# Second attention: the softmax denominators summed on VectorE instead of in a wide product, one step a batch

## The reference, cut to what matters

```python
q = q * scale
sim = jnp.einsum('bhid,bhjd->bhij', q, k)
attn = _softmax(sim)
out = jnp.einsum('bhij,bhjd->bhid', attn, v)
out = jnp.transpose(out, (0, 2, 1, 3)).reshape(b, n, DIM_INNER)
return out @ w_out
```

## Time and profile before

| | us |
|---|---|
| median of 3 runs | 1093.25 (1093.06 to 1094.26) |
| the profiled execution | 1093.4 |
| its span in the trace | 1091.2 |
| PE busy | 1078.2 |
| DVE busy | 797.2 |
| POOL busy | 796.1 |
| ACT busy | 590.6 |
| PE matmuls of the denominators (L1619) | 128 instructions of 592 ns, which overlap in time |
| DVE inversions (L1955) | 119.5, 128 of 934 ns |

### The profile page before, as it was taken

How to read it: one execution, slowest core, us unless ns; L and a number is a source line. 1 busy time by engine, 2 the same in 40 slices (tenths; PEclk the granted TensorE clock), 3 DMA queues, 4 the chain that set the end, 5 groups by cost and what they waited for, 6 DMA issues and landing times.

```text
span 1091.2 us, 22061 instructions
## 1 busy us (share of the span) xinstructions
PE 1078.2 (99%) x8783; PEld 685.0 (63%) x8783; DVE 797.2 (73%) x1247; ACT 590.6 (54%) x939; POOL 796.1 (73%) x524
## 2 busy tenths in 40 slices
PE   9999999999999999999999999999999999999998
PEld 7898998877745455455455455455455545467886
DVE  4658866476675877877877878878878877895553
ACT  4634453576665555555555555655655655654442
POOL 5789998644467899898898899899899898950000
PEclk9999999999999999999999999999999999999999
DMA  7323333200000000200000000000000000000000
GB/s 257 129 79 99 114 103 99 78 1 1 1 1 2 1 1 2 105 4 1 1 1 1 2 1 2 1 1 2 1 1 2 1 2 1 2 0 11 11 1 20
DMA packets 26870, 31.10 MB, mean 28 GB/s; under 512 B 3345, under 2 KB 23185, under 8 KB 25489
## 3 DMA queue, kind: packets, MB, share of 16 engines
q1 hardware_dynamic: 26448, 29.69, 8.1%
q10 hardware_dynamic: 320, 0.01, 0.0%
HBM read 20.12 MB, written 9.44 MB: 27 GB/s over the span
## 4 chain that ended last, share of the span: by engine, by line
PE 90%; DVE 5%; POOL 2%; ACT 2%; issue 1%; SPq 0%; DMA 0%; DVEq 0%; POOLq 0%; ACTq 0%
PE o_ps L1722 21%; PE mx_ps L1675 7%; PE st_ps L1694 5%; PE st_ps L1700 5%; PE st_ps L1697 5%; PE ha_banks L651 4%; PE bank L2127 3%; PE bank L2129 3%; PE bank L2128 3%; PE mx_ps L1613 3%; PE pj_ps L1627 3%; PE pj_ps L1619 2%; PE ha_banks L704 2%; PE ha_banks L715 2%; PE mx_ps L1607 2%
## 5 line engine op out<-in xcount | busy, mean ns | idle before, releaser
L2040 POOL TENSOR_TENSOR acc<-acc,prob 128x1024 f32<-128x1024 f32 x192 | 468.6, 2441 | 49.0 <-ACT prob L1867 38.8
L1867 ACT ACTIVATE prob<-st_ps 128x1024 f32<-128x1024 f32 x256 | 248.6, 1023 | 197.7 <-PE st_ps L1706 104.0
L1722 PE MATMUL o_ps<-prob,v_cur 128*64 128x512 f32 x1024 | 246.4, 602 | 0.0
L1930 DVE TENSOR_REDUCE mx_part<-mx_ps 128x1 f32<-128x512 f32 x258 | 164.8, 666 | 58.0 <-PE mx_ps L1675 58.0
L1933 DVE TENSOR_REDUCE mx_part<-mx_ps 128x2 f32<-128x1024 f32 x78 | 93.6, 1200 | 62.0 <-PE mx_ps L1675 62.0
L1722 PEld LDWEIGHTS o_ps<-prob,v_cur 128*64 128x64 f32 x1024 | 63.8, 136 | 108.9 <-issue 72.8
L1955 DVE RECIPROCAL rden<-rden 128x128 f32<-128x128 f32 x128 | 119.5, 934 | 0.0
L1675 PEld LDWEIGHTS mx_ps<-k_hi,q_hi 64*128 64x128 f32 x414 | 46.5, 183 | 106.7 <-issue 72.6
L1675 PE MATMUL mx_ps<-k_hi,q_hi 64*128 64x512 f32 x414 | 111.9, 457 | 1.2 <-DVE mx_part L1933 0.6
L2040 POOL TENSOR_TENSOR acc<-prob 128x1024 f32<-128x1024 f32 x32 | 76.7, 2397 | 33.9 <-ACT prob L1867 33.3
L1700 PE MATMUL st_ps<-q_hi,d_lo 64*128 64x512 f32 x512 | 100.9, 390 | 0.0
(11 more groups left out here) (414 smaller groups left out, 2266.2 us busy)
## 6 DMA issues: line engine op xcount, KB each, us to landing
v_rows<-ha_v SPq DMA_DIRECT2D x8, 1024.0 KB, 4.1
ha_vt<-v_rows SPq DMA_DIRECT2D x16, 512.0 KB, 4.0
q_max<-mx_turned SPq DMA_DIRECT2D x128, 1.0 KB
h_w<-in_h SPq DMA_DIRECT2D x2, 1024.0 KB, 8.0
w_raw<-in_w SPq DMA_DIRECT2D x8, 192.0 KB, 3.4
head_wkv<-in_wkv SPq DMA_DIRECT2D x2, 512.0 KB, 5.8
m_w<-in_m SPq DMA_DIRECT2D x3, 256.0 KB, 2.9
out<-fin SPq DMA_DIRECT2D x3, 256.0 KB, 2.2
```

The source lines that it names most:

```text
L1722: mm = pe.matmul(o_ps[rows(h), :], v_cur[:, m % 2, j, rows(h)], prob[:, (16 * m + slot) % RING, h, :], start=(j == 0), stop=(j == KT - 1), ...
L1867: act.activation(prob[:, n % RING, :, :], st_ps[:, slot % 2, :, :], ACT.Exp, scale=SCALE).then_inc(s_exp, 1)
L1930: dve.reduce_max(mx_part[:, h, i, keys:keys + 1], maxima_banks(q, n)[h], AX_X).then_inc(s_mxr, 1)
L2040: pool.tensor_tensor(total, old, new, ALU.add).then_inc(s_acc, 1)
```

## The change

The denominator is now made in these pieces, for each half of each step:

1. turn: VectorE transposes `acc` [128 x 1024] in blocks of 32x32 into `turned`;
2. sum: VectorE sums each 32 columns of `turned`, which gives `den_part` [128 x 32];
3. PE multiplies `den_part` (16 columns a head) with `lanes`, a matrix that adds up the four blocks of 32 partitions and repeats the result, 4 records of 16 columns in the place of 4 of 512;
4. ACT copies 128x16 to `den_out` in the place of 128x512;
5. back: VectorE inverts 128x16, and transposes it, repeated 32 times, into `rden` [128 x 512].

The places move. VectorE: turn of half 1 (of the step before) in batch 1, its sum in 2, back in 3; turn of half 0 in batch 4, sum in 5, back in 6; both normalisations now in 6 (half 1 of the step before) and 7 (half 0 of this step). PE: the den of half 1 goes from batch 1 to 2, that of half 0 stays in batch 5. POOL's first add of a half now waits for the turn, not for the product. The order after the last step is another: "out" of half 0 comes where the last den stood, the last den after the first hidden layer, the last "out" after two blocks of the second.

```diff
+    LANES, DEN = 32, CH // 32
+    turned = early.sb("turned", [P, 2 * CH])
...
-    INVERT = {6: (0, 0, 0), 7: (0, 1, 0), 0: (0, 2, -1), 1: (0, 3, -1),
-              2: (1, 0, -1), 3: (1, 1, -1), 4: (1, 2, -1), 5: (1, 3, -1)}
+    DEN_TURN, DEN_SUM, DEN_BACK = {1: (1, -1), 4: (0, 0)}, {2: (1, -1), 5: (0, 0)}, {3: (1, -1), 6: (0, 0)}
+    NORMALIZE = {6: (1, -1), 7: (0, 0)}
...
-    AFTER = {1: ("den", 1), 3: ("out", 0), 5: ("den", 0), 7: ("out", 1)}
+    AFTER = {2: ("den", 1), 3: ("out", 0), 5: ("den", 0), 7: ("out", 1)}
+    AFTER_END = {1: ("out", 0), 2: ("den", 1), 7: ("out", 1)}
...
         elif u[0] == "den":
-            half = u[1]
-            pe.wait_ge(s_acc, ADDS * q + 7 * (half + 1))
+            pe.wait_ge(s_turns, den_done(q, u[1], "summed"))
             for h in range(2):
-                mm = pe.matmul(pj_ps[rows(h), :], c.ones[:, 0:HD], acc[:, half, h, :],
+                mm = pe.matmul(pj_ps[rows(h), 0:DEN], lanes[:, :], den_part[:, h * DEN:h * DEN + DEN],
                                start=True, stop=True, skip_group_check=True)
...
-            act.activation(rden[:, half, :], pj_ps[:, :], ACT.Copy).then_inc(s_den, 1)
+            act.activation(den_out[:, :], pj_ps[:, 0:DEN], ACT.Copy).then_inc(s_den, 1)
...
+    def vector_den_turn(dve, q, half):
...
+        dve.wait_ge(s_acc, ADDS * q + 7 * (half + 1))
+        dve.transpose(turned[:, :], acc[:, half, :, :].rearrange("p h n -> p (h n)")).then_inc(s_turns, 1)
+
+    def vector_den_sum(dve, q, half):
+        dve.wait_ge(s_turns, den_done(q, half, "turned"))
...
+        dve.reduce_sum(den_part[:, :], turned[:, :].rearrange("p (n r) -> p n r", r=LANES), AX_X).then_inc(s_turns, 1)
+
+    def vector_den_back(dve, q, half):
+        dve.wait_ge(s_den, 2 * q + half + 1)
+        if q:
+            dve.wait_ge(s_on, 2 * (q - 1) + half + 1)
+        dve.reciprocal(den_rcp[:, :], den_out[:, :]).then_inc(s_turns, 1)
+        dve.wait_ge(s_turns, den_done(q, half, "inverse"))
+        dve.transpose(rden[:, half, :].rearrange("p (n r) -> p n r", r=LANES),
+                      den_rcp[:, :].unsqueeze(2).to_broadcast([P, DEN, LANES])).then_inc(s_turns, 1)
...
-        vector_invert(dve, m, b)
+        if den_at(DEN_SUM, m, b):
+            vector_den_sum(dve, *den_at(DEN_SUM, m, b))
         at_b = before(m, b)
         if second:
             vector_maxima(dve, *second)
         if at_b and at_b[1][0] == "qk":
             vector_low(dve, *at_b)
-        if b == 1 and m >= 1:
-            vector_normalize(dve, m - 1, 0)
-        if b == 5 and m >= 1:
-            vector_normalize(dve, m - 1, 1)
+        if den_at(DEN_TURN, m, b):
+            vector_den_turn(dve, *den_at(DEN_TURN, m, b))
+        if den_at(DEN_BACK, m, b):
+            vector_den_back(dve, *den_at(DEN_BACK, m, b))
+        if den_at(NORMALIZE, m, b):
+            vector_normalize(dve, *den_at(NORMALIZE, m, b))
...
             if m:
-                pool.wait_ge(s_pj, count_of[m - 1, ("den", half)])
+                pool.wait_ge(s_turns, den_done(m - 1, half, "turned"))
```

More of the change, by code:

```diff
@@ L1422, in second_attention, with den_done @@
     ADDS = 14
-    RCPS = 4
-    INVERT = {6: (0, 0, 0), 7: (0, 1, 0), 0: (0, 2, -1), 1: (0, 3, -1),
-              2: (1, 0, -1), 3: (1, 1, -1), 4: (1, 2, -1), 5: (1, 3, -1)}
+    DEN_STEPS = {name: n + 1 for n, name in enumerate(("turned", "summed", "inverse", "back"))}
+    def den_done(q, half, name):
+        return len(DEN_STEPS) * (2 * q + half) + DEN_STEPS[name]
+    DEN_TURN, DEN_SUM, DEN_BACK = {1: (1, -1), 4: (0, 0)}, {2: (1, -1), 5: (0, 0)}, {3: (1, -1), 6: (0, 0)}
+    NORMALIZE = {6: (1, -1), 7: (0, 0)}
     QK = (("qk", 1, 0), ("qk", 0, 0), ("qk", 0, 1), ("qk", 1, 1))
@@ L1454, in after @@
     def after(m, b):
-        if b not in AFTER:
-            return None
-        q = m + AHEAD[AFTER[b]]
-        return (q, AFTER[b]) if 0 <= q < STEPS else None
+        places = AFTER if m < STEPS else AFTER_END
+        if b not in places:
+            return None
+        q = m + AHEAD[places[b]]
+        return (q, places[b]) if 0 <= q < STEPS else None
     def maximum(m, b, second):
@@ L1825, in scalar_unit @@
             half = u[1]
[L1826 to L1827 removed]
+            if q or half:
+                was = 2 * q + half - 1
+                act.wait_ge(s_turns, den_done(was // 2, was % 2, "inverse"))
             act.wait_ge(s_pj, count_of[q, u])
[L1829 removed]
+            act.activation(den_out[:, :], pj_ps[:, 0:DEN], ACT.Copy).then_inc(s_den, 1)
     def scalar_differences(act, q):
@@ L1891, in vector_start @@
         dve.memset(mx_part[:, :, :, :], 0.0).then_inc(s_rowfill, 1)
+        for h in range(2):
+            dve.reduce_sum(lanes[:, h * LANES:h * LANES + LANES], c.ident[:, :].rearrange("p (n r) -> p r n", r=LANES), AX_X)\
+               .then_inc(s_rowfill, 1)
     def vector_split(dve, p):
@@ L1944, in vector_maxima, with den_at @@
             dve.transpose(mx_turned[:, :], mx_row[:, :].bitcast(F32)).then_inc(s_turned, 1)
[L1946 to L1955, removed]
+    def den_at(places, m, b):
+        if b not in places or m == STEPS:
+            return None
+        half, ahead = places[b]
+        return (m + ahead, half) if 0 <= m + ahead < STEPS else None
+    def vector_den_turn(dve, q, half):
+        if q or half:
+            was = 2 * q + half - 1
+            dve.wait_ge(s_turns, den_done(was // 2, was % 2, "summed"))
+        dve.wait_ge(s_acc, ADDS * q + 7 * (half + 1))
+        dve.transpose(turned[:, :], acc[:, half, :, :].rearrange("p h n -> p (h n)")).then_inc(s_turns, 1)
+    def vector_den_sum(dve, q, half):
+        dve.wait_ge(s_turns, den_done(q, half, "turned"))
+        if q or half:
+            dve.wait_ge(s_pj, count_of[(q, ("den", 0)) if half else (q - 1, ("den", 1))])
+        dve.reduce_sum(den_part[:, :], turned[:, :].rearrange("p (n r) -> p n r", r=LANES), AX_X).then_inc(s_turns, 1)
[7 more added lines that the diff above has]
+                      den_rcp[:, :].unsqueeze(2).to_broadcast([P, DEN, LANES])).then_inc(s_turns, 1)
     def vector_normalize(dve, q, half):
@@ L1960, in vector_normalize @@
         dve.wait_ge(s_osum, 2 * q + half + 1)
-        dve.wait_ge(s_rcp, RCPS * (2 * q + half + 1))
+        dve.wait_ge(s_turns, den_done(q, half, "back"))
         dve.tensor_tensor(o_n[:, half, :], o_sum[:, half, :], rden[:, half, :], ALU.mult).then_inc(s_on, 1)
@@ L1984, in vector @@
         was = (m, b - 1) if b else (m - 1, BATCHES - 1)
-        if after(*was) and AFTER[was[1]][0] == "out":
+        if after(*was) and after(*was)[1][0] == "out":
             vector_add_out(dve, *after(*was))
@@ L2465, in _ @@
                 t2.tensor(pe, STEPS, 1)
[L2466 to L2470, removed]
+                for m in range(HT):
+                    end.tensor_hidden(pe, 0, 1, m)
+                t2.tensor(pe, STEPS, 2)
                 end.tensor_hidden(pe, 0, 2, 0)
+                end.tensor_hidden(pe, 0, 2, 1)
                 t2.tensor(pe, STEPS, 7)
@@ L2479, in _ @@
                         for m in range(HT):
-                            if (k, layer) != (0, 1) and (k, layer, m) != (0, 2, 0):
+                            if (k, layer) != (0, 1) and (k, layer, m) not in ((0, 2, 0), (0, 2, 1)):
                                 end.tensor_hidden(pe, k, layer, m)
```

24 lines of the change are left out of this document (16 added, 8 removed).

## The result

The changed kernel takes 1102.91 us (median of four executions, 1101.22 to 1104.72) against 1093.76 us for the kernel before (1093.06 to 1094.34): ratio 1.0084, 95% interval 1.0065 to 1.0103. It is slower by 9.15 us. The forecast was +23.4. The profiled execution of after is the longest of its four, 1104.72 us, with a span of 1102.5 us.

The account below looks back on a forecast made before the run. PE, busy 99%, was taken to bound the kernel if DVE and POOL deliver; step 0 -0.6, steps 1 to 7 and 14 +9.6, steps 8 to 13 +9.2, last step +5.8, after it -0.6: +23.4 on 1093.4, 1117 us; range 1082 to 1125.

Parts of the forecast that it names:

- The 0.05 us a step for batches 1 and 4: DVE, batches 1 and 4: turns end within 0.2 us of the next first set, costing 0.05 us a step.
- The mechanism: Batch 6: the normalisation misses POOL's add boundary by 0.36 us, waits for that add, and PE waits 2.37 us.
- The wait of the last step: Last step: PE's den waits 5.5 us for DVE's sum, queued behind x_hi, x_lo and h_lo; 1.8 to 6.9 possible.
- +5.2 for the last step and the end: Last step +5.8 from the den's wait, dens and tiles left to split; after it -0.6 for a cheaper last den.
- By the same sum it misses by a hair: Steps 8 to 13, batch 6: normalisation ready 0.03 us after POOL's add begins, so +1.53 a step, +9.2 in all.
- rival (a): Steps 8 to 13: the normalisation gets in ahead of POOL's add, -5.7 there; +8.5 in all, 1102 us; chance 0.20.
- Step 7: Booked with steps 1 to 7 and 14: batch 6's normalisation waits for POOL's add, +1.2 us a step.
- Steps 1 to 6 and 14: Booked with step 7: -1.22 for dens, +0.05 for batches 1 and 4, +2.37 for PE's wait; +1.2 a step.
- rival (e): Last step: PE's clock falls in the long wait, slowing the matmuls behind; +2 to +4 us on any case, no chance given.
- (b): Batch 6, all steps: the normalisation gets in ahead of POOL's add, the way back being shorter; 1085 us; chance 0.18.
- (c): Whole kernel: DVE has room everywhere and PE's saving of 19.5 us is all there is; 1074 us; chance 0.07.
- (d): Batches 1 and 4: turns cost 0.057 us per 32 columns and overrun, +1.35 a step; 1136 us; chance 0.08.

Follow-up runs that it names:

- experiment 3: The changed kernel with half 1's normalisation moved from batch 6 to batch 5, and the last step's sum directly behind its turn, four h_lo tiles later: 1071.91 us.
- experiment 5: The changed kernel with unneeded matmuls ahead of PE's waits, six in batch 7 of steps 1 to 6 and 14, 22 before the last step's den: 1094.72 us.
- experiment 6: The changed kernel with an unread POOL add of 72 columns ahead of d_lo in steps 1 to 6 and 14: 1085.25 us.
- experiment 2: The changed kernel with the last step's half 0 sum directly behind its turn and the four h_lo tiles moved into the network behind: 1094.09 us.
- experiment 7: The kernel of experiment 3 with every transpose of `acc` made twice, in batches 1 and 4 of each step: 1119.66 us.

## Why the prediction was right in its parts and too high in its sum

**Right, by its own steps.** The turn takes 1.24 to 1.25 us (1.25 predicted), the sum 1.21 (1.20), the inversion 0.24 (0.25), the way back 0.71 (0.71). Between the two sizes of transpose lie (1.24 - 0.71) / 512 = 1.04 ns an element, close to the 1.02 of the reductions (1.20 less 0.17 us for 1008 elements more), so the rate was rightly taken from them. The Trainium skill, "Vector Engine (DVE) Microarchitecture Reference", section 3.8, says that the transposing array sustains one element per cycle and lane; the trace agrees in that its slope is nearly the same for both kinds of instruction; how long a cycle is, no run here shows. The 0.05 us a step for batches 1 and 4 holds: the first half of a step loses 0.70 (21.40 to 20.70 from batch 0 to batch 4), and in experiment 3 the second half loses 0.77, each about what the den gives. The mechanism was named rightly: a normalisation that misses POOL's boundary in batch 6, ends 0.54 after the next one (561.48, measured 0.54), and delays the first set of batch 7. Its price too: PE's V unit was to come 2.37 us later, and it comes 2.33 later in step 5 of after than in step 5 of experiment 3 (37.94 against 35.61 us from the start of the step's first score product), though PE shows only 1.95 of it as a wait. The wait of the last step was put at 5.5 us and measured 6.4. That +5.2 for the last step and the end meets the measured +5.5 is partly luck: up to the first product of the network the step gives +7.4, of which 2.3 are the clock that the sum did not have, and the end gives -1.9, where +5.8 and -0.6 were booked.

**The step that failed: "By the same sum it misses by a hair".** Steps 8 to 13 were booked with +1.53 each, +9.2; they gave -1.12 each, -6.7. That is 15.9 us too much, where the whole sum is 12.1 too high (+23.4 against +11.3 of span); the other errors go both ways and give 3.8 back. The normalisation was put 0.03 us behind POOL's add; it is 0.20 ahead of it, and takes 0.80 us. For the chain of step 4 and step 5, both counted from the start of POOL's pair of adds (501.70 in the prediction, 551.97 in the trace of after):

| | predicted | measured |
|---|---|---|
| second set starts | 4.79 | 4.61 |
| normalisation ready | 7.02 | 6.73 |
| POOL's next add begins | 6.66 | 6.57 |
| late by | 0.36 | 0.16 |

Two terms make up the 0.29 on the normalisation. The den that lies between the two chains costs less than the 0.25 booked: a half shortened by 0.70, not by 0.61, so 0.86 - 0.70 = 0.16 is left of it. And I put a handover of 0.03 behind the way back, where the next instruction's listed start lies 0.08 before the way back's listed end (558.07 + 0.71 = 558.78, next 558.70), 0.11 together. The remaining 0.09 I can't assign. POOL's boundary was 0.09 earlier than my sum of single durations; the difference is 0.20. The text knew that 0.1 us decided, gave the tie to the late side by 0.03, and so had a coin's toss for its likeliest case. What happened in these steps is rival (a), which had a chance of 0.20 and the time of 1102. That its 1102 is near the measured time is luck: its +8.5 holds nothing for the clock, and without the clock the change is only 1.15 us slower (experiment 5). So its other terms were some 7 us too high, and the clock, which it left out, cost some 8.

**Step 7** was also booked late (+1.2) and came in (-1.2). Its adds of batch 5 start 0.28 later than those of step 5, counted from the start of the step (637.73 - 610.99 = 26.74; 551.97 - 525.51 = 26.46), at the same time of ACT's exponentials. In before it is already another step than those ahead of it (the same delay of 0.29; its normalisation takes 1.87, in steps 1 to 6 and 14 1.60), so the prediction could have seen it. In eight of the nine traces, a load of instructions (queue q14) falls some 0.6 us behind the start of these adds, and the delay is there; in experiment 6, with more instructions on POOL, none falls there, and the delay is gone. That fits, but only as a coincidence; that the load is the cause isn't shown.

**Steps 1 to 6 and 14** are 0.87 longer than before where +1.2 was booked (step 1 some 0.5 more, in every kernel here but before). The stall was sized right, so the difference is the den: -1.44 a step in experiment 3, where I had -1.22 and 0.05 back.

**The clock** was in the sum nowhere, and in the range for the last step only (rival (e), 2 to 4 us; 2.3 measured, 168.4 against 170.7). For the waits of about 2 us I had no such term, and they cost some 1.7 in four of seven steps, 6.9 us. In the profiled execution step 0 adds 1.5: +0.8 rather than -0.6 (the clock stood at 0.79 from 308 to 316 us there, behind a wait of 1.36 us; before has that wait too, 1.31, without the fall; experiment 2 has 1.00 and 43.0 us). By experiment 5 the change without the clock's share is 1.15 us slower than before (1094.72 against 1093.57).

**The rivals.** (b) and (c) are excluded in after: the way back takes 0.71, and seven steps have the late normalisation. The time of (c), 1074, is near what experiment 3 gives (1071.9), once one normalisation stands a batch earlier and the last sum directly behind its turn; its reason, "DVE has room everywhere", is not, since experiment 7 shows no room behind the turns. (d) is excluded by the 1.24 of the turn. (e) came, and in more places than it named.

The sum, line by line, against the profiled execution and its span:

| us | forecast | measured |
|---|---|---|
| start and step 0 | -0.6 | +0.2 (1.5 of it the clock) |
| steps 1 to 6 and 14, without the clock | +8.4 | +6.6 |
| the clock in steps 1, 2, 4 and 6 | 0 | +6.9 |
| step 7 | +1.2 | -1.2 |
| steps 8 to 13 | +9.2 | -6.7 |
| last step and end | +5.2 | +5.5 (2.3 of it the clock) |
| sum | +23.4 | +11.3 |

**What stays open.** When the clock falls: with the same 1.94 to 1.96 us of idle it fell in steps 1, 2, 4 and 6 and not in 3, 5 and 14, in after and in experiment 2 alike. In step 0, behind a wait of 1.31 to 1.39 us, it fell in three of the nine traces (after, experiments 5 and 7). Experiment 5 shows that filling the gap prevents the fall in the seven steps, not what decides between them. The part of the change that is another order at the end was not run alone: from the first product of the network to the end are 130.4 us before and 128.5 after, 1.9 less, of which the den (about 0.7) and a wait of 0.34 are accounted for.

## What to carry to other kernels

The normalisation, a VectorE instruction with two operands in SBUF, had no duration of its own beside GpSimd's instructions, which read two operands in SBUF as well: it took 0.68 to 2.89 us and always ended 0.55 us after the end of the GpSimd instruction that ran when it became ready. So put such an instruction in a batch that can bear a whole GpSimd instruction ahead of it, before asking how much work is moved. Where a sum of durations puts it within 0.3 us of such a boundary, treat both outcomes as equally likely and time the neighbouring places. And when another engine comes to wait for a result, look at what stands ahead of that result in the queue: here three tiles between turn and sum made PE wait 6.4 us for a product that had cost it 0.96.

## What the runs showed of the hardware that I had not expected

- An idle time of PE of 1.94 to 1.96 us, the only long one in its step, was followed by some 4 us at half the full clock (0.50 from 606 to 608 us in step 6), in four of seven like places; six small matmuls (twelve records) in the gap prevented it in all (41.84 to 41.88 us in steps 2 to 6 and 14).
- All 268 normalisations that started while GpSimd ran ended 0.546 to 0.558 us after the end of GpSimd's instruction. The transposes of 128x1024 took 1.23 to 1.25 us in all eight traces that have them, beside the same GpSimd adds.
- More work on GpSimd (0.34 us in each of seven steps) made the kernel 17.7 us faster, and an untouched step 3.6 us slower.
- A den product of four records with 64-wide weights and 16 columns costs PE 0.18 us from start to start; eight records of one column and 128-wide weights take 0.98.
- VectorE's cast of 128x512, an instruction with one operand, took longer beside GpSimd's adds as well: x_hi took 1.37 us in after and 2.58 in experiment 2, against 0.45.
